# One attention-and-FFN layer: the early order of Pool and TensorE, the x scale at a slot's end, and an FFN lag of 4 slots in place of 5

## The reference

```python
def _mlstm_cell(q, k, v, igate_w, igate_b, fgate_w, fgate_b, ln_scale):
    ifg = jnp.concatenate([q, k, v], axis=-1)
    ig = (ifg @ igate_w.T + igate_b).T
    fg = (ifg @ fgate_w.T + fgate_b).T
    log_f = jax.nn.log_sigmoid(fg)
    cs = jnp.cumsum(log_f, axis=1)
    log_D = where(causal, cs[:, :, None] - cs[:, None, :], -inf) + ig[:, None, :]
    max_log_D = jnp.max(log_D, axis=-1, keepdims=True)
    C = qk / sqrt(DH) * jnp.exp(log_D - max_log_D)          # 8 heads of 16
    normalizer = jnp.maximum(jnp.abs(C.sum(-1, keepdims=True)), jnp.exp(-max_log_D))
    h = (C / (normalizer + EPS)) @ vh
    return (h - mean(h)) / sqrt(var(h) + LN_EPS) * ln_scale

x = x + mlstm(layernorm(x), ctx, ctx, ...)
h = s0 * ([n, -n] @ sign(k0)), n = layernorm(x)
h = s1 * ((2 * relu(h)) @ sign(k1))
x = x + s2 * ((2 * relu(h)) @ sign(k2))
```

## Time and profile before

| | |
|---|---|
| median of 3 runs | 131.81 us (131.75 to 132.53) |
| the profiled execution | 130.65 us |
| its span on the core | 128.9 us |
| mean granted TensorE clock | 0.972 |
| busy: PE, DVE, ACT, POOL | 108.4, 100.7, 74.0, 70.7 us |

### The profile page before, as it was taken

One profiled execution on the slowest core, in us unless ns is written; L12 is line 12 of the kernel. 1 busy time (PEld: TensorE's weight loads), 2 busy tenths in 40 slices (PEclk: granted clock), 3 DMA queues, 4 the chain that ended last, 5 costly groups with the idle time before them and its releaser, 6 DMA issues.

```text
span 128.9 us, 3323 instructions
## 1 busy us (share of the span) xinstructions
PE 108.4 (84%) x1123; PEld 77.6 (60%) x1123; DVE 100.7 (78%) x294; ACT 74.0 (57%) x173; POOL 70.7 (55%) x143
## 2 busy tenths in 40 slices
PE   4989999993899585896898999999999979798961
PEld 4867658572555243564484674856747649586950
DVE  5786589828986999992899999999999989654541
ACT  3045885973495696227957773792694273747120
POOL 5595885187778389781675688687151333340000
PEclk9999999999658999999999999999999999999999
DMA  3645182139853838558129476674600100100101
GB/s 100 181 107 159 36 238 70 42 52 186 156 95 69 154 85 156 98 104 139 29 22 200 83 169 100 122 151 74 135 0 5 41 0 5 41 27 14 44 2 41
DMA packets 12992, 11.38 MB, mean 88 GB/s; under 512 B 2080, under 2 KB 11440, under 8 KB 12976
## 3 DMA queue, kind: packets, MB, share of 16 engines
q0 software_dynamic: 1728, 6.29, 26.8%
q1 hardware_dynamic: 10112, 4.53, 13.6%
q10 hardware_dynamic: 1136, 0.35, 1.2%
HBM read 8.94 MB, written 1.25 MB: 79 GB/s over the span
## 4 chain that ended last, share of the span: by engine, by line
PE 53%; ACT 14%; DVE 12%; issue 10%; POOL 5%; DMA 3%; SPq 1%; DVEq 0%; ACTq 0%; POOLq 0%
PE pF L455 19%; PE pS L381 9%; PE pF L434 5%; PE pO L395 4%; PE pO L402 3%; ACT dmat L594 3%; DVE h L872 3%; PE pF L366 3%; PE pG L343 3%; ACT h L645 3%; ACT oT L617 3%; DMA bias_in<-in_L_xattn_fgate_b 3%; PE pF L447 2%; POOL maxb L996 2%; POOL maxb L1001 1%
## 5 line engine op out<-in xcount | busy, mean ns | idle before, releaser
L455 PE MATMUL pF<-h,w 128*128 128x256 f16 x256 | 30.5, 273 | 1.2 <-DVE h L872 1.2
L872 DVE SCALAR_TENSOR_TENSOR h<-pF,h 128x512 f16<-128x512 f32 x32 | 21.5, 683 | 10.7 <-ACT h L645 10.6
L645 ACT ACTIVATE h<-pF 128x512 f16<-128x512 f32 x32 | 18.1, 594 | 19.9 <-PE pF L455 19.9
L455 PEld LDWEIGHTS pF<-h,w 128*128 128x128 f16 x256 | 24.5, 98 | 4.3 <-DVE h L872 1.3
L1029 POOL TENSOR_TENSOR x2p<-x,x2p 128x128 f16<-128x128 f32 x16 | 9.1, 569 | 19.0 <-ACT x2p L631 18.9
L785 DVE SCALAR_TENSOR_TENSOR cmat<-pS,dmat 128x1024 f32<-128x1024 f32 x15 | 18.2, 1215 | 1.1 <-PE pS L381 1.1
L381 PE MATMUL pS<-q_heads,qcT 64*128 64x512 f32 x64 | 19.0, 672 | 0.0
L996 POOL TENSOR_SCALAR_AFFINE_SELECT maxb<-aT 128x1024 f32<-128x1024 f32 x12 | 13.3, 1107 | 4.1 <-ACT em L575 4.1
L395 PEld LDWEIGHTS pO<-cmat,vals 128*32 128x32 f32 x256 | 6.4, 112 | 12.8 <-issue 10.3
L1001 POOL DMA_DIRECT2D maxb<-running_max x12 | 11.4, 953 | 3.6 <-POOL maxb L996 3.6
L395 PE MATMUL pO<-cmat,vals 128*32 128x128 f32 x256 | 10.5, 283 | 3.5 <-POOL vals L986 2.2
(11 more groups left out here) (124 smaller groups left out, 198.2 us busy)
## 6 DMA issues: line engine op xcount, KB each, us to landing
maxb<-running_max POOLq DMA_DIRECT2D x12, 512.0 KB, 5.2
out<-outb SPq DMA_DIRECT2D x8, 128.0 KB, 2.3
xs<-in_x SPq DMA_DIRECT2D x3, 256.0 KB, 3.3
cs_in<-in_ctx SPq DMA_DIRECT2D x3, 256.0 KB, 4.1
q_heads<-qcT SPq DMA_DIRECT2D x24, 32.0 KB, 2.7
xs<-in_x SPq DMA_DIRECT2D x2, 128.0 KB, 3.2
cs_in<-in_ctx ACTq DMA_DIRECT2D x1, 256.0 KB, 3.6
k_in<-in_L_ffn_k SPq DMA_DIRECT2D x1, 256.0 KB, 3.5
```

Of the source, the lines that this page charges most:

```text
L455: last = pe.matmul(bank[:, u], w1[:, k, columns], h1[:, k, part], start=(k == 0 and part == 0), stop=(k == FT - 1 and part == 1))
L645: act.activation(hidden(f, m, 0), ffn_place(f, m), ACT.Relu).then_inc(ffn_high, 1)
L872: dve.scalar_tensor_tensor(out=hidden(f, m, 1), in0=ffn_place(f, m), scalar=0.0, in1=hidden(f, m, 0), op0=ALU.max, op1=ALU.subtract).then_ ...
```

## The change

- `FFN_LAG` is 4: each pair enters the FFN one slot sooner, and there are 22 slots in place of 23. To make that possible x takes one slot less on its way: `norm_x`, `x2_take_high` run for item n-2 in slot n, `x2_take_low` and `turn_x2` for item n-3.
- POOL: `hx_scale` is split. `h_scale(n-2)` stands at the slot's start, `x_scale(n-2)` at its end, behind `place` and `take_values`. Each has an inverse root of its own (one column). The semaphore `hx_rstd` becomes `h_rstd` and `x_rstd`.
- POOL's slot 1 has no `place`; slot 2 has those of items 4 and 5. The normalization of group 2's queries (four `xn`) moves from DVE's slot 1 to POOL, ahead of the slots.
- `gates(g+1)` on PE, its `gate_logs` on ACT and `gate_scans` on DVE move from a slot's start to behind attention and the slot's first FFN sums; `turn_am` comes behind `weigh`, and `gate_out` behind `decay`.

```diff
-FFN_LAG = 5
+FFN_LAG = 4
...
             def turn_late_xn(g):
-                pe.wait_ge(xn_ready, GB * (g + 1))
+                if g == 2:
+                    pe.wait_ge(xn_late, GB)
+                else:
+                    pe.wait_ge(xn_ready, GB * g)
...
-                if prepare and k == 0 and n > 0:
-                    gates(g + 1)
                 if 0 < n < B:
                     scores(n)
...
-                if prepare and k == 1 and g > 0:
-                    turn_am(g + 1)
                 if k == 3 and g + 2 < NG:
                     turn_late_ctx(g + 2)
                 if 0 <= n - 1 < B:
                     weigh(n - 1)
+                if prepare and k == 1 and g > 0:
+                    turn_am(g + 1)
...
-                if 0 <= n - 4 < B:
-                    turn_x2(n - 4)
+                if 0 <= n - 3 < B:
+                    turn_x2(n - 3)
...
                 for f, m in early:
                     ffn(f, m)
+                if prepare and k == 0 and n > 0:
+                    gates(g + 1)
...
-                if prepare and k == 0 and n > 0:
-                    gate_logs(g + 1)
                 if n == 1:
                     gate_logs(1)
-                if prepare and k == 1 and g > 0:
-                    gate_out(g + 1)
...
+                if prepare and k == 1 and g > 0:
+                    gate_out(g + 1)
                 for f, m in early:
                     high(f, m)
-                if 0 <= n - 3 < B:
-                    norm_x(n - 3)
-                    x2_take_high(n - 3)
+                if prepare and k == 0 and n > 0:
+                    gate_logs(g + 1)
+                if 0 <= n - 2 < B:
+                    norm_x(n - 2)
+                    x2_take_high(n - 2)
...
                 if n == 1:
-                    norm_group(2)
                     gate_scans(1)
-                if prepare and k == 0 and n > 0:
-                    gate_scans(g + 1)
...
                 if behind:
                     h_centred(n - 1)
+                if prepare and k == 0 and n > 0:
+                    gate_scans(g + 1)
...
+            def scale(part, b, signal):
+                e = b % 2
+                step(pool.tensor_scalar(ve_hx[:, e, part:part + 1], mv_hx[:, e, part, 1:2], LN_EPS, X2_SCALE ** -2,
+                                        ALU.add, ALU.mult))
+                pool.tensor_tensor(rs_hx[:, e, part:part + 1], ve_hx[:, e, part:part + 1], minus_half[:, 0:1],
+                                   ALU.pow).then_inc(signal, 1)
+
+            def h_scale(b):
+                pool.wait_ge(h_stats, b + 1)
+                if b >= 2:
+                    pool.wait_ge(x1_ready, b - 1)
+                scale(0, b, h_rstd)
+
+            def x_scale(b):
...
+                pool.wait_ge(x_stats, b + 1)
+                if b >= 2:
+                    pool.wait_ge(x2_ready, b - 1)
+                scale(1, b, x_rstd)
+                pool.wait_ge(x_rstd, b + 1)
+                pool.tensor_scalar(nb_x[:, e:e + 1], mv_hx[:, e, 1, 0:1], rs_hx[:, e, 1:2], -1.0,
+                                   ALU.mult, ALU.mult).then_inc(x_shift, 1)
...
             q_scale(2 * GB, GB)
+            pool.wait_ge(q_rstd, 3 * GB)
+            pool.wait_ge(turned, 3)
+            for n in range(2 * GB, 3 * GB):
+                pool.tensor_scalar(xn[:, n % (2 * GB)], xs[:, n], mv_q[:, n, 0:1], rs_q[:, n:n + 1], ALU.subtract,
+                                   ALU.mult).then_inc(xn_late, 1)
             q_scale(3 * GB, GB)
             for n in range(SLOTS):
-                if 0 <= n - 4 < B:
-                    x2_take_low(n - 4)
-                if 0 <= n - 2 < B + 1:
-                    hx_scale(n - 1)
-                place(n + LEAD)
+                if 0 <= n - 3 < B:
+                    x2_take_low(n - 3)
+                if 0 <= n - 2 < B:
+                    h_scale(n - 2)
+                for i in (() if n == 1 else (GB, GB + 1) if n == 2 else (n + LEAD,)):
+                    place(i)
                 take_values(n + GB)
+                if 0 <= n - 2 < B:
+                    x_scale(n - 2)
```

More of the change, by code:

```diff
@@ L177, in xattn_ffn @@
         xn_ready = sem("xn_ready")
+        xn_late = sem("xn_late")
         vals_ready = sem("vals_ready")
@@ L206, in xattn_ffn @@
         h_centre = sem("h_centre")
-        hx_rstd = sem("hx_rstd")
+        h_rstd = sem("h_rstd")
+        x_rstd = sem("x_rstd")
         x_stats = sem("x_stats")
@@ L738, in norm_q @@
                 dve.wait_ge(q_stats, n + 1)
-                if n >= 2 * GB and n % GB == 0:
-                    dve.wait_ge(turned, 3 if n // GB == 2 else 5)
+                if n == 3 * GB:
+                    dve.wait_ge(turned, 5)
                 e = n % (2 * GB)
@@ L816, in h_moments_of @@
             def h_moments_of(n):
-                return mv_hx[:, (n + 1) % 2, 0]
+                return mv_hx[:, n % 2, 0]
             def x_moments_of(n):
@@ L828, in h_moments @@
                 if n >= 2:
-                    dve.wait_ge(hx_rstd, n - 1)
+                    dve.wait_ge(h_rstd, n - 1)
                 dve.bn_aggr(h_moments_of(n), st_h[:, n % 2]).then_inc(h_stats, 1)
@@ L843, in residual @@
                 dve.wait_ge(h_centre, n + 1)
-                dve.wait_ge(hx_rstd, n + 1)
+                dve.wait_ge(h_rstd, n + 1)
                 if n >= XR:
                     dve.wait_ge(x2_ready, n - XR + 1)
-                dve.scalar_tensor_tensor(out=x1[:, n % XR], in0=hsc[:, n % 2], scalar=rs_hx[:, (n + 1) % 2, 0:1],
+                dve.scalar_tensor_tensor(out=x1[:, n % XR], in0=hsc[:, n % 2], scalar=rs_hx[:, n % 2, 0:1],
                                          in1=xs[:, n], op0=ALU.mult, op1=ALU.add).then_inc(x1_ready, 1)
@@ L1002, in place @@
                                accum_op=ALU.add).then_inc(max_spread[g % 2][j], 16)
-            def hx_scale(n):
-                e = n % 2
-                has_h, has_x = 0 <= n - 1 < B, 0 <= n - 2 < B
-                part = slice(0 if has_h else 1, 2 if has_x else 1)
-                if has_h:
-                    pool.wait_ge(h_stats, n)
-                if has_x:
-                    pool.wait_ge(x_stats, n - 1)
-                if n >= 3:
-                    pool.wait_ge(x1_ready, n - 2)
-                if n >= 4:
-                    pool.wait_ge(x2_ready, n - 3)
-                step(pool.tensor_scalar(ve_hx[:, e, part], mv_hx[:, e, part, 1], LN_EPS, X2_SCALE ** -2, ALU.add, ALU.mult))
-                pool.tensor_tensor(rs_hx[:, e, part], ve_hx[:, e, part], minus_half[:, 0:part.stop - part.start],
-                                   ALU.pow).then_inc(hx_rstd, 1)
-                if has_x:
-                    pool.wait_ge(hx_rstd, n)
-                    pool.tensor_scalar(nb_x[:, e:e + 1], mv_hx[:, e, 1, 0:1], rs_hx[:, e, 1:2], -1.0,
-                                       ALU.mult, ALU.mult).then_inc(x_shift, 1)
+            def scale(part, b, signal):
[10 more added lines that the diff above has]
+            def x_scale(b):
+                e = b % 2
+                pool.wait_ge(x_stats, b + 1)
[5 more added lines that the diff above has]
+                                   ALU.mult, ALU.mult).then_inc(x_shift, 1)
             def x2_take_low(n):
```

## The result

| | before | changed |
|---|---|---|
| median | 131.78 us (130.73 to 132.53, 4 runs) | 142.54 us (141.62 to 143.51, 4 runs) |
| ratio, 95% interval | | 1.084 [1.077, 1.091] |
| profiled execution, span | 130.65, 128.9 us | 143.51, 141.8 us |
| mean granted TensorE clock | 0.972 | 0.940 |

The forecast was 139.5 us in a range of 134.5 to 144.0, with a chance of 0.90 that it is slower. The time lies in the range, 3.0 us above the forecast.

The account below looks back on a forecast made before the run. PE was taken to bound the kernel from slot 9, no engine in slots 3 to 8. Start 32.9, nine slots of 6.18, gate waits, later slots and tail gave span 137.3, median 140.2, rounded to 139.5; range 134.5 to 144.0 us.

Parts of the forecast that it names:

- The ring of POOL and ACT: POOL's low half waits for ACT's cast, which needs POOL's x_scale: 6.18 us per full slot, slots 3 to 11.
- The split's share of the ring: In POOL's slot, splitting the scales costs 0.8 us of the 6.18.
- Where it starts: POOL's low half of item 0, low(0), in slot 3, was put at 32.9 us.
- The query norms on POOL: Ahead of POOL's first place: 1.7 to 2.4 us, zero on the path, up to 0.5 if the cover failed.
- The wait in slot 3: PE stands from the end of weigh(2) at 30.4 to 33.3, some 3 us.
- The gate waits: POOL's place(8) and place(12) wait for gate_out in slots 5 and 9: about 2.3 and 1.7 us, 4.0 together.
- Slots 12 to 15: Slot 12, without a copy, 5.6 us; slots 13 to 15, paced through all three engines, 5.6 on average.
- The tail: Behind slot 15, two slots of 4.4 us; from the last x transposes to the end unchanged at 13.07 us.
- POOL's port: DVE's residual beside a mask on POOL takes up to 0.75 us more each; nothing added to the forecast.
- Rival 1: Nothing measurable: no gate waits, 5.2 us in slots 13 to 15, tail as before; 133.0 us by the median, chance 0.07.
- Rival 2: Faster: POOL is early enough and PE sets the pace, 6.6 us less, 125.2 us; chance 0.05.
- Rival 3: Slower still: PE's waits of 1 to 3 us per slot lower its clock, three stretches, 146.5 us; chance 0.10.

Follow-up runs that it names:

- split_early_order: Changed kernel with x and the FFN back one slot (lag 5) and the gates back in front: 131.50 us, ratio 1.001 to before.
- L: Part of the change: x and the FFN one slot sooner; the changed kernel without it ran at 138.99 us, ratio 1.058 to before.
- gates_in_front: Changed kernel with the gates back at a slot's front on PE, ACT and DVE: 140.94 us, ratio 1.073 to before.
- P: Part of the change: the split of the scales, with that of x at the slot's end; not run alone.
- early_order: Kernel before with the early places and the four query norms on POOL alone: 130.05 us, ratio 0.987.
- early_places: Kernel before with the early places alone (none in slot 1, two in slot 2), query norms still on DVE: 129.57 us, ratio 0.985.
- gates_behind: Kernel before with only the gates, their logarithms, scans and output moved behind attention: 131.28 us, ratio 1.000.
- G: Part of the change: the gates behind attention; alone in the kernel before, 131.28 us, ratio 1.000.
- E: Part of the change: the early places and the query norms on POOL; alone in the kernel before, 130.05 us, ratio 0.987.
- G with P: Kernel before with the late gates and the split scales, that of x at the slot's end: 136.34 us, no ratio.
- x_slot_later: Changed kernel with x and the FFN back on the old schedule (FFN_LAG 5), all else kept: 138.99 us, ratio 1.058 to before.

## Why the prediction was right, point by point

Its mechanism, sign and main term stand; how near the time came is in part luck, as the end of this section says. From the profiled execution, forecast (span 137.3) against result (141.8):

- *The ring of POOL and ACT*, 6.18 for each full slot: 6.18 between 56.64, 62.82 and 69.00, and again between 83.41, 89.59 and 95.77. Right, and shown by split_early_order, where L alone is undone against gates_in_front. In the other five slots it was 0.15 to 0.47 longer, 1.4 in all (the gate waits apart): `nb_x` took up to 0.74 for 0.26, and ACT's cast came once 0.3 later (1.24 at 75.59). The prediction had each row at its undisturbed length.
- *The split's share of the ring*, 0.8 us: by the prediction's own rows it is 0.7 (0.83 + 1.20, less the 1.35 from 49.46 to 50.81). L without P was not run. The copy's share, taken as 0.60 from its row, was 0.28.
- *Where it starts*: 32.9 forecast, 34.96 measured. 1.36 of that is the later start of the whole, which nothing in the argument knew; from the first place to the low half it was 7.40 us (27.56 to 34.96) for 7.00, as the second of two masks in a row took 1.38.
- *The query norms on POOL*: 1.7 to 2.4 us, an estimate without a row of its form, and they took 3.33:

```profile
21.21 3.33 POOL L1083 TENSOR_SCALAR xn<-xs,mv_q,rs_q 128x128 f32<-128x128 f32 x4
...
26.77 0.19 POOL L1010 TENSOR_SCALAR ve_hx<-mv_hx 128x1 f32<-128x1 f32 x1 [0.18 <-DVE mv_hx L835]
```

  The cover of 4.05 us was just enough: POOL still waited 0.18 for DVE behind them. Zero on the path was right, as early_order and early_places show with equal spans.
- *The wait in slot 3*, about 3 us: 3.44.
- *The gate waits*, 2.3 and 1.7, together 4.0: 2.27 and 1.49, together 3.76. Here they cost their full length, the low halves behind them coming 8.70 and 7.82 us after the ones before. gates_behind shows that the same waits cost nothing where POOL has room, so the condition (in the ring) carried the term. Undoing G brought back 1.6 to 2.2 us and not 3.8, since x one slot sooner delays `gate_out` by itself.
- *Slots 12 to 15*, four times 5.6: 5.86, 5.88, 5.30, 5.89 (22.9 for 22.4). Right, with the alternation where it was said.
- *The tail*, two of 4.4: 4.65 and 4.76; the end from the last x transposes 13.1 for 13.1 (141.8 - 128.68).
- *POOL's port*, nothing added: the residual took 0.61 to 1.09 us for four of the 16 items (28.19, 36.41, 43.06, 78.87) and at most 0.44 for the others. POOL's scales of x up to slot 11 (32.81 to 93.63) have no idle time in front of them, so zero was right.
- *Signs named*: the low halves, the masks' waits and the 3 us in slot 3 came. Scores "over 6 us apart to slot 12 and over 5.3 behind it" did so with two exceptions, 5.21 from slot 11 to 12 and 5.27 from 14 to 15.
- *Rival 1* gave slots 3 to 12 at their old length. low(0) to low(9) took 60.8 us. Wrong by its gate waits, and by its tail.
- *Rival 2* fails on the ring. Its gain in slot 3 exists, though: early_places is that gain with the ring left out.
- *Rival 3*: the stretches came (four of them) and cost nothing beside the ring.

So the span was undersized by 4.5 us: the start (2.1), the ring's disturbed slots (1.4), slots 12 to 15 and the tail (1.2), less 0.2 of gate waits. That the median is only 3.0 us above the forecast is luck: the prediction put it 2.9 us above the span, as in before, but here the profiled execution was the longest of four and the median is 0.7 above its span; the rounding down took 0.7 the other way. The prediction's own terms reach up to 139.5 + 2.5 = 142.0 us. The result, 142.54, lies in the 2.0 us up to 144.0 for which no term is given.

The one thing the prediction had no word for is that G and P hold a second loss of several us behind the ring. It came out only with the ring open; that in the changed kernel the ring covers it, both being waits for POOL at the same places, is an argument and not shown. Undoing L alone gave back 3.5 of the 10.8 us, undoing G alone 1.6, and undoing both 11.0: their shares don't add.

## What to carry to other kernels

Before a producer is moved to the end of one queue's slot and its consumer kept at the head of the next, go once round the ring through the other engines and sum starts: the total is the new slot's length however idle each engine looks. Undo parts of a slow change in pairs: here one part alone (G) and one pair (P with E) were level with before while another pair (G with P) cost some 4 us, and the smallest part held a gain of 1.5%. Level isn't free either: the gain of E hid the price of P.

## What the runs showed of the hardware that was not expected

DVE's normalizations can lose a microsecond at once beside POOL. In before the pair shown here began 0.45 us ahead of POOL's fill of `vals`; in the changed kernel it began 0.3 us later, 0.15 ahead of the fill:

```profile
6.90 0.60 DVE L742 TENSOR_SCALAR xn<-xs,mv_q,rs_q 128x128 f32<-128x128 f32 x2
```

```profile
7.17 1.26 DVE L747 TENSOR_SCALAR xn<-xs,mv_q,rs_q 128x128 f32<-128x128 f32 x2
...
7.32 0.96 POOL L1068 MEMSET vals<- 128x1024 f32 x1
```

0.60 against 1.26 us, and the pair ended with the fill, at 8.43 and 8.28. In early_places one such instruction took 2.27 us beside a DMA issue and a mask of POOL, where 0.37 stood in before, at 30.65:

```profile
27.28 2.27 DVE L742 TENSOR_SCALAR xn<-xs,mv_q,rs_q 128x128 f32<-128x128 f32 x1
```

It ended at 29.55, and POOL's second mask in a row (28.07 and 1.38 long) at 29.45. The Trainium skill (SBUF — State Buffer, Who interferes with whom) says that DVE's `tensor_scalar` can enter a mode that takes the port pair it shares with GpSimd, and that whichever engine comes second for the pair blocks for the whole instruction of the first; that both DVE rows end within 0.15 us of POOL's agrees with it.

The moving start of the first scan has another cause for the most part. In nine of the fourteen kernels the scan starts at 11.5 to 12.6 us, in the other five at 10.6 to 10.7, in both groups with and without each part of the change; that is why the table takes it off. Only three of the nine have the slow pair (the changed kernel, x_slot_later and gates_in_front, at 12.03 to 12.60). What all nine share is slow rows on PE. Transposes and gate products ahead of the scan, in before and in split_early_order:

```profile
6.57 0.60 PE L313 MATMUL pG<-ident,cs_in 128*128 128x128 f32 x4
...
8.55 0.42 PE L343 MATMUL pG<-qcT,wkv 128*32 128x128 f32 x8
```

```profile
6.79 1.06 PE L315 MATMUL pG<-ident,cs_in 128*128 128x128 f32 x4
...
9.06 0.66 PE L348 MATMUL pG<-qcT,wkv 128*32 128x128 f32 x8
```

The five early kernels have the first pair of lengths, eight of the nine late ones the second. The changed kernel has 0.60 for the transposes and then 0.65 to 0.68 for the gate products, where its granted clock reads 0.50 (10 to 12 us). So 0.66 is what the products take at the low level of TensorE's clock, and the eight kernels look like it from the start on, though their granted clock reads 1.00 there; why they start so isn't shown.
